# Reordering a transformer block's batch loop: scores and values of one batch beside the next batch's cross-attention, feed-forward beside its maxima

## The reference

```python
x = x + cross_attention(layernorm(x), ctx)      # 16 heads of 64, 64 keys
n = layernorm(x)
# dense path, causal self-attention with 16 heads of 16 channels
o = softmax(causal(q @ k.T / 4)) @ v            # q, k, v = n @ wq, n @ wk, n @ wv
h = n + rmsnorm(o @ wo)
dense = h + rmsnorm((silu(h @ w1) * (h @ w3)) @ w2)      # inner width 1024
# sparse path, 8 experts, the best two of each token
sparse = rmsnorm(sum(gate[k] * expert[k](n) for k in top2(softmax(n @ router_w))))
return x + dense + sparse
```

## Time and profile before

| what | value |
|---|---|
| median of 3 runs | 1718.03 us (1711.98 to 1718.67) |
| the profiled execution | 1725.52 us |
| its span | 1723.7 us |
| PE busy | 1407.8 us (82%) |
| DVE busy | 845.5 us (49%) |
| ACT busy | 543.7 us (32%) |
| POOL busy | 503.4 us (29%) |
| mean granted clock of PE | 0.914 |

### The profile page before, as it was taken

The page is one execution under the profiler, slowest core; times in us unless marked ns, Lnnn a source line. Parts: engine busy times, 40 slices in busy tenths (PEclk is TensorE's granted clock), DMA queues, the critical chain, the costliest instruction groups (busy, mean ns, idle before and its releaser), DMA issues.

```text
span 1723.7 us, 25491 instructions
## 1 busy us (share of the span) xinstructions
PE 1407.8 (82%) x7721; PEld 955.2 (55%) x7722; DVE 845.5 (49%) x1877; ACT 543.7 (32%) x1018; POOL 503.4 (29%) x680
## 2 busy tenths in 40 slices
PE   7765896899788978897889789878978789999930
PEld 3542565567555755675467556655655465666620
DVE  0445463646464546545555556454636423333347
ACT  3230532152225214430532053215321413333322
POOL 3123043204411340323032303330432013555532
PEclk9885999899889989998999889989997889999975
DMA  5314105010501050014102310401040352222247
GB/s 215 127 49 87 26 1 125 10 38 0 131 4 37 2 129 19 21 35 99 38 1 61 74 38 0 105 30 38 1 122 13 114 87 68 85 85 85 86 165 256
DMA packets 107072, 116.68 MB, mean 68 GB/s; under 512 B 39416, under 2 KB 80912, under 8 KB 107024
## 3 DMA queue, kind: packets, MB, share of 16 engines
q1 hardware_dynamic: 88080, 98.10, 20.3%
q0 software_dynamic: 8576, 17.87, 3.3%
q10 hardware_dynamic: 10368, 0.04, 0.3%
HBM read 71.36 MB, written 44.21 MB: 67 GB/s over the span
## 4 chain that ended last, share of the span: by engine, by line
PE 56%; issue 19%; DMA 7%; POOL 5%; DVE 5%; SPq 4%; ACT 3%; ACTq 0%; POOLq 0%; DVEq 0%
PE ps L892 9%; PE ps L925 7%; PE ps L763 6%; DMA room<-parts_d 5%; PE ps L746 5%; PE ps L900 5%; PE ps L775 3%; PE ps L942 3%; PE ps L813 3%; SPq L436 3%; PE ps L715 2%; PE ps L877 2%; PE ps L734 2%; PE ps L668 2%; PE ps L687 2%
## 5 line engine op out<-in xcount | busy, mean ns | idle before, releaser
L813 PE MATMUL ps<-room 96*128 96x128 bf16 (+3 forms) x512 | 151.2, 353 | 118.3 <-DMA room<-parts_d 88.1
L892 PE MATMUL ps<-hT,w 128*128 128x512 f32 x768 | 205.6, 418 | 9.7 <-DVE gT L1406 8.3
L1055 ACT ACTIVATE room<-ps 128x1024 f32<-128x1024 f32 x160 | 159.5, 1023 | 143.5 <-PE ps L847 140.0
L1355 DVE TENSOR_REDUCE nm<-ps 128x2 f32<-128x256 f32 (+3 forms) x160 | 127.0, 823 | 104.7 <-PE ps L814 101.8
L892 PEld LDWEIGHTS ps<-hT,w 128*128 128x128 f32 x768 | 148.1, 196 | 47.0 <-DVE gT L1406 9.0
L813 PEld LDWEIGHTS ps<-room 96*128 96x128 bf16 x512 | 55.0, 108 | 180.7 <-issue 119.3
L1077 ACT ACTIVATE th<-ps 128x512 f32<-128x512 f32 x64 | 38.3, 598 | 364.5 <-PE ps L892 364.5
L925 PE MATMUL ps<-room 128*128 x288 | 137.2, 599 | 3.5 <-ACT room L1092 3.5
L845 PE MATMUL ps<-room 99*128 99x512 bf16 (+3 forms) x512 | 127.0, 323 | 8.9 <-DMA room<-mT 6.3
L900 PE MATMUL ps<-w,gT 128*128 128x256 f32 x512 | 121.4, 380 | 0.4 <-DVE gT L1406 0.4
L562 POOL TENSOR_TENSOR ve_a<-mv,eps 128x1 f32<-128x1 f32 (+1 forms) x40 | 9.9, 247 | 376.5 <-DVE mv L1240 247.7
(11 more groups left out here) (216 smaller groups left out, 2554.7 us busy)
## 6 DMA issues: line engine op xcount, KB each, us to landing
room<-parts_d SPq DMA_DIRECT2D x96, 256.0 KB, 7.0
room<-xs_d SPq DMA_DIRECT2D x72, 128.0 KB, 2.0
room<-pair_d SPq DMA_DIRECT2D x8, 1024.0 KB, 7.5
room<-in_L_ffn_ew SPq DMA_DIRECT2D x24, 256.0 KB, 6.2
xin<-in_x SPq DMA_DIRECT2D x8, 512.0 KB, 4.0
parts_d<-xnT SPq DMA_DIRECT2D x32, 128.0 KB, 1.8
parts_d<-o_tok SPq DMA_DIRECT2D x32, 128.0 KB, 1.8
parts_d<-oT SPq DMA_DIRECT2D x32, 128.0 KB, 1.7
```

Of the source, the lines that this page charges most:

```text
L813: mm(bank(o, n), q_rep[0:KREP, rep_at(h), t * P:n], k_rep[0:KREP, rep_at(h), 0:n], start=True, stop=False)
L892: last = mm(bank(up_banks(b, m)[i]), w[:, x, k, m * P:(m + 1) * P], hT[:, y, k, :], start=((x, y, k) == terms[0]), stop=((x, y, k) == term ...
L1055: done(fn(prob[:, grp % 2, u * 1024:(u + 1) * 1024], ps[:, n % 2 * 1024:n % 2 * 1024 + 1024], ACT.Exp), "b_exp")
L1355: done(v.tensor_reduce(nm[:, t, 2 * hp:2 * hp + 2], pair_ps, AX.X, ALU.max, negate=True), "a_max")
```

## The change

`STEPS` is written anew. Score, value and `out_t` steps now work on batch c, as the net's steps do, and stand between the steps of batch b's cross-attention. The whole feed-forward net of c moves behind it, to the projections, the routing and the maxima of batch b. All 32 `max` steps of b stand in the second half of the iteration. In detail:

- Scores are made in 40 units of at most 512 columns in banks 6 and 7; ACT's exponentials are 512 wide. `prob` has one buffer instead of two. A group's value products come in three chunks `va`.
- Cross-attention's steps `m`, `bqk`, `vw`, `cs`, `ct`, `cv`, and `qk`, `v`, `route` are cut into smaller steps.
- Maxima all use the pairs in banks 0 to 3; there are two shifts instead of three.
- `th`, `gT`, `oT`, two of the three `parts` and others move into `room`. hT lies over the start of `room`, where `m_sb` is; hb is a new tile: POOL copies the second norm into it (`f_hb`), then `h` and `y` are made there, and a sum `z` = x1 + xn is made at the end of the iteration.
- SP copies the shift rows of c at the start of the iteration, behind the load of x. Before the experts, SP first zeroes the padding rows and then loads the experts' weights, where it was the other way round.
- The split of w1 and w3 into two terms in the first batch moves from `qk` and `v` to `route`.

The diff, cut to its core:

```diff
+def scores_of(grp):
+    order = [("sc", grp, u) for u in range(6)] + [("va", grp, 0)]
+    order += [("sc", grp, u) for u in range(6, 9)] + [("va", grp, 1), ("sc", grp, 9)]
+    return order
+
+SCORES = []
+for _g in range(G):
+    SCORES += scores_of(_g)[:2] if _g else scores_of(0)[:2]
+    SCORES += [("va", _g - 1, 2)] if _g else []
+    SCORES += scores_of(_g)[2:5]
+    SCORES += [("out_t", _g - 1)] if _g else []
+    SCORES += scores_of(_g)[5:]
+SCORES += [("va", G - 1, 2)]
+
+CROSS = [
+    ("x_turn",), ("m", 0), ("m", 1), ("f_hb",), ("m", 2), ("m", 3), ("bqk", 0), ("bqk", 1),
+    ("cs", 0, 0), ("cs", 0, 1), ("vw", 0), ("vw", 1), ("exp", 0), ("vw", 2), ("vw", 3), ("sum", 0), ("x_bias",),
+    ("cs", 1, 0), ("cs", 1, 1), ("exp", 1), ("sum", 1), ("ct", 0, 0), ("ct", 0, 1),
+    ("cs", 2, 0), ("cs", 2, 1), ("exp", 2), ("cv", 0, 0), ("cv", 0, 1), ("sum", 2), ("ct", 1, 0), ("ct", 1, 1),
+    ("cs", 3, 0), ("cs", 3, 1), ("exp", 3), ("cv", 1, 0), ("cv", 1, 1), ("sum", 3), ("ct", 2, 0), ("ct", 2, 1),
+    ("cv", 2, 0), ("cv", 2, 1), ("ct", 3, 0), ("ct", 3, 1), ("cv", 3, 0), ("cv", 3, 1), ("norm_3",),
+]
+def interleaved():
+    first, rest = SCORES[:6], SCORES[6:]
+    slots = [i for i, s in enumerate(CROSS) if s[0] in ON_PE and s[:2] != ("cv", 3)]
+    order, given = [("x_norm",)] + first, 0
+    for i, s in enumerate(CROSS):
+        order.append(s)
+        if i in slots:
+            want = (slots.index(i) + 1) * len(rest) // len(slots)
+            order += rest[given:want]
+            given = want
+    return order
...
-    ("fu", 2), ("x2_turn",), ("qk",), ("v",), ("route",), ("fu", 3), ("fd", 2), ("slots",), ("fu", 4), ("fd", 3),
-    *maxima(0), ("fu", 5), ("fd", 4), *maxima(1), ("fu", 6), ("fd", 5), *maxima(2),
-    ("fu", 7), ("fd", 6), *maxima(3), ("shift_parts", 0), ("fd", 7), ("shift", 0),
-    *maxima(4)[:2], ("f_end",), *maxima(4)[2:], ("f_scale",),
...
+STEPS = interleaved() + [
+    ("out_t", G - 1), ("f_o_turn",), ("x2_turn",), ("f_wo",), ("qk", 0), ("qk", 1), ("f_o_norm",), ("qk", 2), ("qk", 3),
+    ("v", 0), ("v", 1), ("v", 2), ("v", 3), ("route", 0), ("f_h_turn",), ("route", 1), ("fu", 0), ("f_yb",), ("route", 2),
+    ("fu", 1), ("fd", 0), ("slots",), ("fu", 2), ("fd", 1), ("scatter",),
+    ("fu", 3), *maxima(0), ("fd", 2), ("fu", 4), *maxima(1), ("fd", 3), ("fu", 5), *maxima(2), ("fd", 4), ("fu", 6), *maxima(3),
+    ("shift_parts", 0), ("fd", 5), ("fu", 7), ("shift", 0), *maxima(4), ("fd", 6), *maxima(5)[:2], ("fd", 7), *maxima(5)[2:],
+    *maxima(6)[:2], ("f_end",), *maxima(6)[2:], *maxima(7)[:2], ("f_scale",), *maxima(7)[2:], ("z",), ("shift_parts", 1), ("shift", 1),
 ]
+OF_PREVIOUS = ("f", "sc", "va", "out_t")
...
             def batch(b, c):
                 if b is not None:
...
                     if c is not None:
                         load_x(b)
                     else:
                         load_late_weights()
+                if c is not None:
+                    for i, (first_head, end_head) in enumerate(SHIFTS):
+                        need(sp, c, "mT_sb", i + 1)
+                        for r in range(MROWS):
+                            done(sp.dma_start(q_rep[KREP + r:KREP + r + 1, rep_at(first_head):rep_at(end_head - 1) + 1:KD, :],
+                                              mT[r * H + first_head:r * H + end_head, i, :]), f"m_row{i}", 16)
...
-                    for i, (first_head, end_head) in enumerate(SHIFTS):
-                        need(sp, b, "mT_sb", i + 1)
-                        for r in range(MROWS):
-                            done(sp.dma_start(q_rep[KREP + r:KREP + r + 1, rep_at(first_head):rep_at(end_head - 1) + 1:KD, :], mT[r * H + first_head:r * H + end_head, i, :]), "m_row", 16)
+                if b is None:
+                    experts_first()
                 if c is not None:
                     need(sp, c, "y", 1)
-                    done(sp.dma_start(at_batch(y_d, c), yb[:, :, :]), "y_out", 16)
+                    done(sp.dma_start(at_batch(y_d, c), hb[:, :, :]), "y_out", 16)
...
+                    elif step[0] == "f_o_norm":
+                        need(pool, c, "wo_n", 2)
+                        need(pool, c, "hb", 1)
+                        done(g.tensor_tensor(hb[:, :, :], hb[:, :, :], o_tok[:, :, :], ALU.add), "h")
...
+                    elif step[0] == "f_scale":
                         need(pool, c, "fd_n", 1)
                         need(pool, c, "yb", 1)
-                        done(g.tensor_tensor(yb[:, :, :], yb[:, :, :], scaled, ALU.add), "y")
+                        need(pool, c, "hT_ps", 2)
+                        done(g.tensor_tensor(hb[:, :, :], yb[:, :, :], scaled, ALU.add), "y")
...
+                    elif kind == "sc":
...
+                        if n == 0:
+                            before(pe, c, "fd_n")
+                        if u == 0 and grp in (0, 2):
+                            need(pe, c, f"m_row{grp // 2}", 48)
                         if n >= 2:
-                            need(pe, b, "b_exp", n - 1)
+                            need(pe, c, "b_exp", n - 1)
```

More of the change, by code:

```diff
@@ L78 @@
-_late = [s for hp in (5, 6, 7) for s in (maxima(hp)[:2], maxima(hp)[2:3], maxima(hp)[3:])]
-for _g in range(G):
-    for _u in range(5):
-        STEPS += [("score", _g, _u)]
-        if _g and _u == 1:
-            STEPS += [("value", _g - 1)]
-        if _g and _u == 3:
-            STEPS += [("out_t", _g - 1)]
-        if _late:
-            STEPS += _late.pop(0)
-            STEPS += {6: [("shift_parts", 1)], 0: [("shift_parts", 2)]}.get(len(_late), [])
-        STEPS += {(0, 4): [("shift", 1)], (2, 0): [("shift", 2)]}.get((_g, _u), [])
@@ L93, in steps_of, with of_previous @@
+OF_PREVIOUS = ("f", "sc", "va", "out_t")
+def of_previous(step):
+    return step[0][0] == "f" or step[0] in OF_PREVIOUS
 def steps_of(attention, net):
     if attention:
-        return [s for s in STEPS if net or s[0][0] != "f"]
-    order = [("f_out_t", G - 1), ("f_o_turn",), ("f_wo",), ("f_o_norm",), ("f_h_turn",), ("fu", 0)]
+        return [s for s in STEPS if net or not of_previous(s)]
+    order = [("f_hb",)] + SCORES + [("out_t", G - 1), ("f_o_turn",), ("f_wo",), ("f_o_norm",), ("f_h_turn",), ("fu", 0), ("f_yb",)]
@@ L736, in batch @@
                     elif kind == "cs":
-                        t = step[1]
-                        if t == 0:
+                        t, half = step[1:]
+                        if half == 0 and t == 0:
                             need(pe, b, "m_act", 2)
@@ new lines, in batch @@
+                        if half == 0:
+                            need(pe, b, "sc_nrm", t + 1)
+                            if t == 0:
+                                need(pe, b, "vw_sb", 4)
+                        elif t:
+                            need(pe, b, "x1", t)
+                        for a in range(4):
+                            last = tr(bank(2 + half, P, a * P), s_sb[:, t % 2, (half * 4 + a) * P:(half * 4 + a + 1) * P], ident[:, :])
+                        done(last, "pT_ps")
@@ L759, in batch @@
                     elif kind == "cv":
[L760 to L762 removed]
+                        t, half = step[1:]
+                        if half == 0:
+                            need(pe, b, "pT_sb", 2 * t + 2)
+                        for a in range(half * 4, half * 4 + 4):
                             last = mm(bank(3, D), pT[:, t % 2, a * P:(a + 1) * P], vw[:, a, :], start=(a == 0), stop=(a == PAIRS - 1))
[L764 removed]
+                        if half:
+                            done(last, "pv_ps")
@@ L865, in batch @@
-                        done(last, "av_ps")
-                    elif kind == "out_t":
-                        out_t(b, step[1])
-                    elif kind == "f_out_t":
-                        out_t(c, step[1])
+                            need(pe, c, "o_nrm", grp)
+                        for t in range(T):
+                            last = tr(bank(5, P, t * P), av[:, t * P:(t + 1) * P], ident[:, :])
+                        done(last, "avT_ps")
                     elif kind == "f_o_turn":
-                        before(pe, c, "fd_n")
+                        need(pe, c, "b_exp", per["b_exp"])
```

607 lines of the change are left out of this document (283 added, 324 removed), and 2 rows, old and new, of the table STEPS.

## The result

The changed kernel takes 1893.88 us (median of 4 runs, 1883.88 to 1899.11), the kernel before 1716.94 beside it: ratio 1.1029, 95% interval 1.0977 to 1.1081. It is slower, as forecast, but by 177 us and not by 69; 1893.9 lies above the range. The profiled execution takes 1883.88 us, its span is 1882.1 at a mean granted PE clock of 0.877 (0.914 before). It is the fastest of its four runs, and the profiled execution of the kernel before is the slowest of its own, so the two profiles are 158 us apart and not 177.

The account below looks back on a forecast made before the run. PE, busy 82% of the span, was taken as the bound, with 34.5 of 165.3 us an iteration lost. 181.3 + 7 x 176.9 + 81.3 = 1500.9 us for 1431.8, so +69: median 1787 us, range 1710 to 1830.

Parts of the forecast that it names:

- Reads of the parts: From last `cv` to first maximum: 41.3 us, PE's own work to 37.4, the wait falling from 9.71 to 3.9.
- Maxima with net blocks: Rounds of down, up, maxima wait for DVE: 8.35 us each, 1.7 more, 5.1 an iteration over three rounds.
- The clock: Rival: lower clock holds through the maxima, 16.6 us an iteration, 1903 us; within the 0.12 given to longer iterations.
- Maxima without blocks, and `y`: Head pairs 4 to 7 after the net blocks: from 77.1 us, f_scale ends at 92.5, `y` at T = 95.0.
- The turn of the iteration: From `y` to x_turn: x's issue 4.3, its load 3.6, statistics to x_turn 4.7, together 12.7 us exposed.
- 6.4 us if x were early: Low bound for the stretch from `y` to x_turn, leaving DVE's copy and the 4.7 us; 12.7 was taken.
- Cross-attention with scores: From x_turn to last `cv`: PE's work 62.5 us, waits 4.9, half clock 1.75, together 69.2 us.
- The ends: First batch's x_turn at about 181.3 us, formerly 206.0; first expert product 81.3 behind where an eighth x_turn would stand.

Follow-up runs that it names:

- the filled kernel: Changed kernel with products that change nothing (zero weights or idle bank) in PE's waits in the rounds and around the second shift, the lesser filling: 1847.39 us, ratio 1.0747.
- both edits: Changed kernel with up block before down block in each round, and SP's next-batch loads and first shift rows ahead of its wait for `y`: 1796.92 us, ratio 1.0469.
- the kernel with the scores apart: Changed kernel with all score and value units ahead of the next batch's x_turn, none beside cross-attention: 1993.07 us, ratio 1.1303.
- the better kernels: Two successive versions on both edits plus x_norm in the maxima: first more order edits, 1739.69 us; then sum h, exp 1 and sum 1 moved, loop written out, 1679.57 us.
- the first experiment: Changed kernel with only the order of each round swapped back to up, down, maxima: 1883.88 us, ratio 1.0687.
- the first better kernel: On both edits plus x_norm in the maxima, four order edits: up blocks, `z`, av turn with f_wo, six score units ahead of second shift: 1739.69 us, ratio 1.0117.
- all four kernels of this chip: Changed kernel with round order swapped back (1883.88 us), loads early (1938.83), or scores apart (1993.07); kernel before with down block ahead of up block (1806.28).

## Why the prediction was right in its direction and short in its size

An iteration was forecast at 176.9 us and takes 189.8. Of the 12.9 us missing, the iteration shown above (188.4 us) has 5.2 in the maxima with net blocks, 3.6 around the turn and 3.1 in cross-attention, less 0.4 in the reads. The rest is mainly one long round more, which most iterations have.

**Reads of the parts: right in length by luck.** 40.9 us to the first maximum for 41.3, but from two errors that cancel. The wait for the reads, 9.71 us before and forecast at 3.9, is at most 0.9. PE's own work in front of it, summed at 37.4, lasts 40.7 in five of seven iterations, in the iteration shown at a clock of 0.86 in its first 12 us and 0.89 in the next 15. So the wait shrank by more than forecast, and PE's longer work took the difference back.

**Maxima with net blocks: the mechanism right, the size too small.** The term was "8.35 us a round, 1.7 more". Rounds at the upper clock take 8.36, and the filled kernel has them throughout. What failed is that I priced the wait and not what follows it: 19 of 21 rounds have their down block, or part of it, at 1.2 GHz and take some 10.0. With the first pair, and the down block at 1.2 GHz and the wait of 2.31 us in front of the shift, the window is 41.0 us for 35.8, in an iteration with only two long rounds. The clock was among the rivals, with 4.5 us for each of three rounds and 3 on the last pairs; it was 1.7 a round and little on the last pairs. That this rival's total, 1903 us, is near the measured 1894 is luck: the rest of the miss lies in the turn and in cross-attention. The Trainium skill (TensorE: Matmul & The Clock Gate, A second HAM failure mode: psum-queue depth-cycling) says that short idle times between groups of products bring the clock down again and again. Here the traces agree: the clock is down behind most pauses of 1.88 us, and stays up where they are filled; with pauses of 0.61 us the clock stays up. I had held today's rounds against the page, but PE pauses 0.18 us in them and not 1.88:

```profile
810.25 0.34 PE L813 MATMUL ps<-room 96*128 96x384 bf16 x1 [0.18 <-DVE nm L1355]
```

**Maxima without blocks, and `y`: right within 1 us.** 19.0 us from pair 4 to `y` for 17.9.

**The turn of the iteration: the chain right, its cause wrong.** "12.7 us" are 15.1, as the load took 5.4 us for 3.6 and x_norm 5.5 for 4.7. But loading x early gained only 1 to 2 us. Behind the load stood the loop's turn on DVE and PE, behind that x_norm, and beside both the score units with their own turn of the loop. The bound "6.4 us if x were early" was wrong: x_turn stood 12.9 us behind the write of `y` with both edits. The Trainium skill (DMA: Bandwidth & Descriptors, Rules for kernel authors) asks for the early load; the runs agree in sign, but the early load alone is worth some 2 of the 15.1 us.

**Cross-attention with scores: a term mis-sized.** PE is busy 68.6 us at clock 0.97, which is 66.5 at full clock, where I had summed 62.5. Of these 4 us 0.4 are a slip (the items taken out of rows 3 leave 41.2 us of cross-attention and not 40.8); where the others sit is open. The low clock cost 2.1 us for 1.75. The waits were 0.36 in front of x_turn and 2.39, 0.39 and 0.83 in front of score and value units, less than the 4.9 forecast. That makes 72.3 for 69.2. That interleaving is no loss against standing apart is shown by the kernel with the scores apart.

**The ends: right to 3 us each,** 178.3 for 181.3 and 84.4 for 81.3, and the two misses cancel.

Of the 24 us by which an iteration grew (165.4 to 189.0 and 189.9), 12.5 are settled by the two edits that take them away (11 the order of a round, some half of that by way of the clock, 1 to 2 the loads). The other 11 are in the turn, in the last pairs and in cross-attention; the better kernels take back more than that, but by several edits at once, so their shares stay open.

## What to carry to other kernels

When PE's list interleaves two jobs, write down for each engine behind it what it does between two of its turns: up, down, maxima and down, up, maxima are the same products, and 8 to 11 us an iteration apart, of 165 and 190. Price a pause of PE by what it does to the clock behind it, not by its length. And when a load is taken off a chain, look for what ran in its shadow before counting on the gain: here the turn of the loop, then six units ahead in PE's own order.

## What the runs showed of the hardware

- A pause of 1.88 us in each round mostly brings the granted clock to 1.2 GHz in the following block (19 of 21 rounds), 0.61 us doesn't. It is not certain for a single pause: behind the one at 678.63 in the first experiment the up block takes 3.03 us, at full clock. Products with zero weights in the pause keep 2.4 GHz, and 409 instructions more on PE in six iterations made the kernel 40 us faster.
- The turn of a loop costs 2.5 to 2.8 us on DVE and 3.1 to 3.5 on PE in a loop of this length (with the exception of two turns of 0.59 on PE in the first better kernel). With the loop written out DVE has no pause there and PE one of 0.55. The Trainium skill (Runtime: NRT & Kernel Launch, Instruction fetch mechanics) says that a taken branch to code outside the loaded window must wait for its fetch. The traces agree with such a wait, but no run here varied the length of the loop.
- A cast of 128 x 32 takes 0.18 us on DVE alone and 2.20 to 2.27 beside POOL's sum of 128 x 1024; it ends when the sum ends.
- One chip of four was 2.6% slower for the kernel before (1762.33 for 1717 to 1720), and in kernels of every order ACT and DVE paused there in the first rounds, beside POOL's scatters. In one iteration of the first experiment:

```profile
504.09 0.69 DVE L1422 SCALAR_TENSOR_TENSOR room<-room,ps 128x512 f32<-128x512 f32 x1 [5.79 <-remote]
```

No wait on an instruction of the trace explains it, and the same kernel's undisturbed iteration is 11 us shorter than its others. In all four kernels of this chip the undisturbed iteration is the one in which POOL itself stands still in the middle of its 16 scatters, for 4.9 to 8.1 us:

```profile
680.61 0.95 POOL L642 DMA_INDIRECT ids_d<-ids_now,idx_u  x1 [0.30 <-issue]
686.50 0.97 POOL L640 DMA_INDIRECT xs_d<-xn,idx_u  x1 [4.94 <-issue]
```

The other chips show that break of POOL's in the same iteration, and no such pauses of ACT and DVE in any. So the pauses go with an unbroken row of scatters on this chip; what links them is open.
